# Block 3's small transfers spread, down's banks emptied in two halves, and two casts moved ahead of block 0's search

## The reference, cut to what matters

```
s = silu(x @ w_gate.T)                        # 2752 wide
s[the k = 1376 entries of smallest |s| in each row] = 0
x = layernorm(x + (s * (x @ w_up.T)) @ w_down.T)
lin(x, wq, A, B) = x @ tile(wq, (1, 4)).T + 0.5 * (x @ A.T @ B.T)     # A, B of rank 2
x = layernorm(x + lin(silu(lin(x, w1q, a1, b1)) * lin(x, w3q, a3, b3), w2q, a2, b2))
```

## Time and profile before

| | |
|---|---|
| time, median of 3 runs | 1956.67 us (1955.87 to 1958.53) |
| profiled execution | 1959.35 us, its span 1957.6 us |
| PE busy | 1929.8 us (99%), 9320 matmuls |
| DVE, ACT, POOL busy | 1235.9 us (63%), 730.3 us (37%), 912.9 us (47%) |
| mean granted clock of TensorE | 0.997 |
| load of a w_d or w_gate piece, issue to landing | 2.6 us (median) |

### The profile page before, as it was taken

The page is one execution under the profiler, slowest core; times in us unless marked ns, Lnnn a source line. Parts: engine busy times, 40 slices in busy tenths (PEclk is TensorE's granted clock), DMA queues, the critical chain, the costliest instruction groups (busy, mean ns, idle before and its releaser), DMA issues. The chain is left out here.

```text
span 1957.6 us, 24665 instructions
## 1 busy us (share of the span) xinstructions
PE 1929.8 (99%) x9320; PEld 1618.5 (83%) x9320; DVE 1235.9 (63%) x1823; ACT 730.3 (37%) x1184; POOL 912.9 (47%) x705
## 2 busy tenths in 40 slices
PE   9999999999999999999999999999999999999998
PEld 8897978988789888888988988789788777887776
DVE  2147975689864326897632489865016999469963
ACT  4356444463233336523243463233242332123312
POOL 5446884445545544554464445444473332013310
PEclk9999999999999999999999999999999999999999
DMA  4333333334344333434243334333543132212212
GB/s 145 92 103 92 114 108 86 92 98 140 88 131 132 95 87 106 140 96 134 82 140 94 99 97 140 93 126 90 171 155 103 44 116 100 71 60 72 101 44 86
DMA packets 102114, 203.67 MB, mean 104 GB/s; under 512 B 11492, under 2 KB 27876, under 8 KB 100688
## 3 DMA queue, kind: packets, MB, share of 16 engines
q1 hardware_dynamic: 97384, 185.28, 31.0%
q10 hardware_dynamic: 4608, 16.78, 2.1%
HBM read 185.24 MB, written 16.78 MB: 103 GB/s over the span
## 5 line engine op out<-in xcount | busy, mean ns | idle before, releaser
L514 POOL TENSOR_TENSOR wl<-w_in_place,wh 128x512 fp32r<-128x512 f32 (+2 forms) x552 | 712.9, 1295 | 666.3 <-ACT wh L621 666.0
L621 ACT CAST wh<-w_in_place 128x512 fp32r<-128x512 f32 (+2 forms) x560 | 328.1, 589 | 772.5 <-DMA w_in_place<-in_wu 301.3
L1327 PE MATMUL banks<-wh,xTh 128*128 128x512 f32 (+2 forms) x1536 | 567.6, 370 | 9.7 <-POOL wl L514 5.7
L1329 PE MATMUL banks<-wh,xTl 128*128 128x512 f32 (+2 forms) x1536 | 564.7, 368 | 0.0
L1328 PE MATMUL banks<-wl,xTh 128*128 128x512 f32 (+2 forms) x1536 | 564.5, 368 | 0.0
L1327 PEld LDWEIGHTS banks<-wh,xTh 128*128 128x128 f32 x1536 | 289.1, 188 | 53.5 <-POOL wl L514 8.6
L1329 PEld LDWEIGHTS banks<-wh,xTl 128*128 128x128 f32 x1536 | 289.0, 188 | 40.4
L1328 PEld LDWEIGHTS banks<-wl,xTh 128*128 128x128 f32 x1536 | 289.3, 188 | 39.6
L1327 PE MATMUL banks<-wh,hTh 128*128 128x512 f32 x672 | 263.3, 392 | 4.5 <-POOL wl L514 4.5
L1329 PE MATMUL banks<-wh,hTl 128*128 128x512 f32 x672 | 262.3, 390 | 0.0
L1328 PE MATMUL banks<-wl,hTh 128*128 128x512 f32 x672 | 262.1, 390 | 0.0
(11 more groups left out here) (144 smaller groups left out, 2176.4 us busy)
## 6 DMA issues: line engine op xcount, KB each, us to landing
w_in_place<-in_wd SPq DMA_DIRECT2D x176, 256.0 KB, 2.6
w_in_place<-in_wg SPq DMA_DIRECT2D x128, 256.0 KB, 2.6
w_in_place<-in_wu SPq DMA_DIRECT2D x128, 256.0 KB, 2.6
w_in_place<-in_w SPq DMA_DIRECT2D x54, 256.0 KB, 2.9
x_in_place<-in_xT SPq DMA_DIRECT2D x32, 256.0 KB, 3.8
y<-in_xtok SPq DMA_DIRECT2D x4, 2048.0 KB, 8.0
x<-y ACTq DMA_DIRECT2D x16, 512.0 KB, 4.2
xa<-x SPq DMA_DIRECT2D x16, 512.0 KB, 4.2
```

The lines of the kernel that those rows point to most:

```text
L514: nc.gpsimd.tensor_tensor(lo, landed, hi.bitcast(F32), ALU.subtract).then_inc(done, 1)
L621: nc.scalar.copy(hi, piece).then_inc(hi_done, 1)
L1327: nc.tensor.matmul(dst, ah, bh, start=start, stop=False)
L1329: return nc.tensor.matmul(dst, al, bh, start=False, stop=stop)
```

## The change

In SP's queue `load_b` takes two arguments and issues three of its 18 transfers at a time, after each of the pieces d = 10 to 15 of block 3's down, where all 18 stood after d = 12. In ACT's queue pieces 3 and 4 of up 0 are cast ahead of block 0's search, which then starts with piece 5; the numbers of casts inside and behind the rounds stay. In DVE's queue `take_down` takes n and empties the four banks of one half: n = 0 ahead of the last tile's count in the searches of blocks 1 to 3, n = 1 where all eight were emptied. Behind the last down both halves follow each other. Each half ends with a wait for its own four adds.

```diff
--- before.py
+++ after.py
@@ -414,15 +414,13 @@
                 sp.dma_start(a13s[:, :, :], a13).then_inc(small_in, 16)
                 sp.dma_start(a2raw[:, :, :], a2).then_inc(small_in, 16)
 
-            def load_b():
+            def load_b(g, half):
                 sp.wait_ge(b_zero, 2)
-                for g in range(3):
-                    for i, src in enumerate((b1, b3, b1, b3)):
-                        r0 = UP * i + R * g
-                        sp.dma_start(braw[r0:r0 + R, :], src).then_inc(b_in, 16)
-                    for i in range(2):
-                        r0 = 32 * g + R * i
-                        sp.dma_start(b2raw[r0:r0 + R, :], b2).then_inc(b_in, 16)
+                for i, src in ((0, b1), (1, b3)):
+                    r0 = UP * (2 * half + i) + R * g
+                    sp.dma_start(braw[r0:r0 + R, :], src).then_inc(b_in, 16)
+                r0 = 32 * g + R * half
+                sp.dma_start(b2raw[r0:r0 + R, :], b2).then_inc(b_in, 16)
 
             def load_xa(b, t):
 
@@ -471,8 +469,8 @@
                     load_w2((d - 5) // 2)
                 if d == 8:
                     load_small()
-                if d == 12:
-                    load_b()
+                if 10 <= d < 16:
+                    load_b((d - 10) // 2, d % 2)
                 if d in (14, 16):
                     load_xa(0, (d - 14) // 2)
                 if d == 24:
@@ -736,7 +734,9 @@
             for i in range(3):
                 up_0(i)
             evac(0, NJ - 1)
-            ahead = iter(range(3, NG))
+            for i in range(3, RING):
+                up_0(i)
+            ahead = iter(range(RING, NG))
             search(0, lambda: up_0(next(ahead)), (2, 2, 2, 2, 2, 2))
             for i in ahead:
                 up_0(i)
@@ -930,7 +930,7 @@
                 step(V.tensor_scalar(tc[:, 1, 2:4], sadd[:], 12582912.0, -12582912.0, ALU.add, ALU.add))
                 st.done()
 
-            def search(b, meanwhile=None):
+            def search(b):
 
                 st.done()
 
@@ -978,6 +978,8 @@
                                                 op0=ALU.is_equal, op1=ALU.mult, accum_out=tc[:, 0, t:t + 1]))
                     st.done()
 
+                    if b and t == NT - 1:
+                        take_down(b - 1, 0)
                     step(V.tensor_scalar(junkd[:, :], v[:, t, :], tc[:, 0, t:t + 1], None, ALU.is_lt, ALU.add,
                                          accum_out=tc[:, 1, t:t + 1]))
                 st.done()
@@ -991,8 +993,8 @@
                 step(V.transpose(scr[0:32, 64:96], scr[0:32, 0:32]))
                 st.done()
                 V.tensor_reduce(flag[0:1, 0:1], scr[0:1, 64:96], AX.X, ALU.max).then_inc(flag_ready, 1)
-                if meanwhile is not None:
-                    meanwhile()
+                if b:
+                    take_down(b - 1, 1)
                 dve.wait_ge(flag_ready, b + 1)
                 dve.sem_inc(passed_dve, 1)
                 flagged = dve.value_load(flag[0:1, 0:1].bitcast(I32))
@@ -1057,18 +1059,17 @@
                 es.done_apart(passed_dve)
                 assert es.n == EXACT
 
-            def take_down(b1):
+            def take_down(b1, n):
 
                 dve.wait_ge(x_in, 16 * (b1 + 1))
-                for n in range(2):
-                    for t in range(NT):
-                        if t < NT - 1:
-                            dve.wait_ge(d_done, 6 * b1 + 3 * n + t + 1)
-                        else:
-                            dve.wait_ge(pe_used, down_at(b1) + ND - 1 + n)
-                        s = y[:, t, n * 512:(n + 1) * 512]
-                        V.tensor_tensor(s, banks[2 * t + n][:, :], s, ALU.add).then_inc(d_evac, 1)
-                dve.wait_ge(d_evac, 8 * (b1 + 1))
+                for t in range(NT):
+                    if t < NT - 1:
+                        dve.wait_ge(d_done, 6 * b1 + 3 * n + t + 1)
+                    else:
+                        dve.wait_ge(pe_used, down_at(b1) + ND - 1 + n)
+                    s = y[:, t, n * 512:(n + 1) * 512]
+                    V.tensor_tensor(s, banks[2 * t + n][:, :], s, ALU.add).then_inc(d_evac, 1)
+                dve.wait_ge(d_evac, 8 * b1 + 4 * (n + 1))
 
             def norm_sums(n, tile, tiles=range(NT), whole=slice(0, NT)):
 
@@ -1160,7 +1161,7 @@
                 if b > 1:
                     for j in range(NJ):
                         take_gate(b, j)
-                search(b, lambda: take_down(b - 1))
+                search(b)
                 norm_sums(b - 1, lambda t: y[:, t, :])
                 take_up(b)
 
@@ -1189,7 +1190,8 @@
             V.scalar_tensor_tensor(out=b2s[64:LR, :], in0=b2raw[64:LR, :], scalar=LORA,
                                    in1=b2s[64:LR, :].bitcast(F32), op0=ALU.mult, op1=ALU.subtract).then_inc(b_ready, 1)
             dve.wait_ge(b_ready, 4)
-            take_down(NB - 1)
+            for n in range(2):
+                take_down(NB - 1, n)
 
 
             def fold_x(b, t):
```

## The result

The changed kernel takes 1946.05 us (median of 4 runs, 1945.49 to 1946.83) against 1957.6 us for the kernel before (4 runs, 1955.87 to 1959.6): ratio 0.9941, 95% interval 0.9924 to 0.9958. In a later series, of 6 and 13 runs, it was 1946.20 against 1957.56, 0.9944 (0.9923 to 0.9966). The forecast was 1942.0, in a range of 1938.8 to 1948.0.

A forecast was written before the change was run, and what follows sets the result against it. TensorE was busy 99%, so only its idle and slow-clock time could be won. 7.4 + 4.9 + 2.4 = 14.7 us took the profiled 1959.35 to 1944.6; with the runs' median 2.7 lower, 1942.0, range 1938.8 to 1948.

The forecast's parts named there:

- rival A: Block 0: POOL's work slows DVE's steps, so the casts ahead gain 0 to -1 us; 1944.4 to 1945.5; chance 0.2.
- Rival B: Clock falls for another cause than the stalls: Part 1 gives 4.0, Part 2 3.2, total 1947.1 us; chance 0.08.
- C: Up of blocks 1 and 3 or down of block 3: half the stall stays; 1945 to 1947 us; chance 0.07.
- Part 1: Down's banks, blocks 1 to 3: n = 0 adds before last count end blocks 1 and 3's stalls and low clock, 7.4 us.
- Part 2: Down of block 3: small transfers three at a time remove the 3.21 us stall and its low clock, 4.9 us.
- The term for the slower landing: Down of block 3: each weight piece behind a set of three small transfers lands 0.7 us later, a sixth of 4.05.
- Part 3: Block 0: two more casts ahead of the search remove the 2.44 us stall, with no clock gain, 2.4 us.
- the prediction's price: Block 0: casts wait for loads, u's bank copy (2.0 us) moves into round 4's Signs; search ends 1 to 4 us later.
- The 3.1 us of cover at piece 25: Up of block 0: piece 25, cast behind ACT's wait, is ready at 190.2 and wanted at 193.3.
- D: Block 0: the casts ahead also remove the five small POOL stalls, 5.0 us in all; 1939.4 us; chance 0.06.
- E: Down of block 3: each set of three holds the next piece as the lump did, six stalls; 1971.4 us; chance 0.02.

The follow-up runs named there:

- light kernels: Kernel before and changed kernel, each with POOL's products in block 0 cut to 8 columns per tile; one execution each, 1950.08 and 1942.36 us.
- light changed kernel: Changed kernel with POOL's products in block 0 cut to 8 columns per tile; 1942.36 us in one execution.
- doubled sets: Changed kernel with each small transfer issued twice, six in each gap, the second to rows nothing reads; 1949.40 us in one execution.
- part 1 alone: Kernel before with only the take_down and search edit (n = 0 adds ahead of the last count); 1952.14 us, ratio 0.9961.
- parts 1 and 2: Changed kernel without the two casts moved ahead of block 0's search; 1947.97 us, ratio 0.9941 against the kernel before.

## Why the prediction was right, and which terms were off

The measured 1946.05 us lies in the stated range of 1938.8 to 1948.0, but outside the forecast's own range of 1940 to 1944.2, and above what rival A gives. The two large terms had their mechanism and size right; a smaller term and a step between profile and median were wrong, both in the same direction, and the range was wide enough for that on account of rivals B and C, which did not come.

- **Part 1, 7.4 us: right**, 7.6 by the marks. DVE's order is the one that was worked out:

```profile
491.82 2.63 DVE L1071 TENSOR_TENSOR y<-banks,y 128x512 f32<-128x512 f32 x4 [1.60 <-PE banks L1331]
494.48 3.08 DVE L983 TENSOR_SCALAR_CACHE_REDUCE junkd<-v,tc 128x2752 int8<-128x2752 f32 x1
...
499.85 2.47 DVE L1071 TENSOR_TENSOR y<-banks,y 128x512 f32<-128x512 f32 x4
```

  The adds end at 494.45, and up 1 begins at 496.27 at once. The idle of 1.60 us ahead of them is DVE waiting for down's n = 0 piece, which I had only in block 2; there, DVE now came after it and did not wait. Nothing came of either, as priced. Block 2's own stall, which the kernel before has in some executions, I did not have.
- **Part 2, 4.9 us: right**, 5.1. The term for the slower landing was mis-sized: 0.7 us more a piece, measured 4.2 more at worst (7.2 us from load to cast, against 3.0). That was to be about 3 us for each of d = 13 to 18 and was 3.2, 3.6, 5.3, 7.2, 6.5 and 5.1. Of 5 us of cover 1.5 were left, without a stall.
- **Part 3, 2.4 us: the failed step**, by size. It gave 0.7. That the stall "has its cause in the cast's place alone" is what the light kernels contradict. The stall went, and 1.9 us more of idle than before came up at later pieces, by rival A's mechanism (chance 0.2), though A had nothing left of the gain: of the steps between rounds 4 and 5 (counted from 0), four took 1.2 us each beside POOL, and piece 30 waited behind that threshold. POOL's rows of the changed kernel, then DVE's, the first two of these steps and one that it made alone:

```profile
197.17 1.29 POOL L512 TENSOR_TENSOR wl<-w_in_place,wh 128x512 fp32r<-128x512 f32 x1
198.42 1.29 POOL L541 TENSOR_TENSOR w<-w,s 128x512 f32<-128x512 f32 x1
...
197.27 1.21 DVE L927 TENSOR_SCALAR sadd<-sadd 128x2 f32<-128x2 f32 x1
198.51 1.22 DVE L930 TENSOR_SCALAR tc<-sadd 128x2 f32<-128x2 f32 x1
...
202.61 0.17 DVE L955 TENSOR_TENSOR qa<-hc,lc 128x8 f32<-128x8 f32 x1
```

  POOL's two instructions end at 198.46 and 199.71, and DVE's two steps at 198.48 and 199.73. So it is for all of them: of the steps of L925 to L963 that took over 0.9 us in block 0's search, 20 in the kernel before and 18 in the changed one, each ended 0.01 to 0.03 us after an instruction of POOL. The threshold behind these steps came 5.9 us later than in the kernel before (203.55 against 197.65): 4.1 us by the steps, and 1.8 us because they began later, with the copy of u's banks now inside round 4's Signs, as the prediction's price had it. The light changed kernel has that copy too and no idle at 207, so the copy alone does not make the stall.

  The 3.1 us of cover at piece 25 held; it was the next round that ran out. The search ended 3.9 us later (the mask began at 264.76, not 260.85), at the upper end of the 1 to 4 us that were priced, and the mask was done at 270.98, in time for the transposes at 276.27.
- **The frame.** The sum for the profiled execution was 1944.6 and it came out at 1946.1: part 3 gave 1.7 less, parts 1 and 2 some 0.4 more. I then took 2.7 off for the median of the runs. That was wrong on two counts. The median was that of three runs, and 27 and 13 later runs have theirs higher, at 1959.64 and 1957.56, so a part of the 2.7 lay in the choice of those three. And the distance did not carry over: the changed kernel's profiled execution, 1946.1, is at the median of its runs, since the spread went with the stalls. Without that step the forecast is 1944.6. These two errors, 1.5 and 2.7, make up the 4.1 us between 1942.0 and 1946.05.
- **Rival B** (the clock falls for another reason): no kernel's trace has a fall of the clock inside it without a stall of 1.8 us or more right before, so B did not come. But what stood against it was put too simply: a stall does not always bring a fall.
- **C, D and E** did not come; the doubled sets show where E begins.

## What to carry to other kernels

A stall is gone for good only where its cause is gone: the casts moved ahead cured one wait and left POOL's load, which made the next, while emptying half the banks first and spreading the transfers took their waits away whole. When stalls lower the clock, take their removal from the profiled execution's own time, since its distance from the median can be part of what goes. Before spreading small transfers into a queue, check the slowest landing among the pieces behind them, not the mean.

## What the runs showed of the hardware that was not expected

**A stall's length does not decide whether the clock falls.** Over all traces I count 20 stalls of TensorE of 1.79 to 3.38 us inside the kernel. Behind 12 of them the granted clock fell to the 1.2 GHz level and came back, at a cost of 1.7 us each; behind 8, among them ones of 2.43 and 2.47 us, it stayed at 2.4 GHz. All three over 3 us brought a fall. The same stall of 2.44 us at 190 kept it in one kernel and lost it in another that is the same up to there. Stalls up to 1.6 us brought none. At 190 the clock fell in one of five kernels and at the other places in 11 of 15, so the place may count beside chance; no run here tells. The spread of the runs goes with the stalls: 13 us for the kernel before, 5.0 for part 1 alone (two long stalls left), 1.8 for parts 1 and 2 (one left) and 0.8 to 1.3 for the changed kernel, in 27 to 4 runs. The falls are a part of that spread and not the whole: between mean clocks of 0.998 and 0.995 lie about 6 us, where the 13 runs lie 13.5 apart. Stalls that some executions have and others have not, as in block 2, can make up more; no run here splits the rest.

**A two-row transfer holds up what is behind it.** Eighteen of them slowed the next piece's landing from 3.0 to 7.05 us; about the same bytes to 128 partitions did not (3.15), but took SP 0.47 us each to issue where the two-row ones took 0.30. The Trainium skill's page DMA: Bandwidth & Descriptors (Why a DMA increments its semaphore by 16 and not by 1) says that a transfer runs on the largest number of engines up to 16 that divides its slowest dimension, two for these; the DMA share of 0.12 while they ran agrees.
